# Two projection slabs loaded during normalization, halved weight staging, and a second d_gated buffer in an eight-core transformer layer

## The chip, the cores and the metric

The program runs on all 8 cores of one Trainium2 chip, each core with its own 2048 tokens and no exchange between cores. The metric is device time in microseconds (us), that of the slowest core. PE is TensorE (matmuls), DVE is VectorE, ACT is ScalarE, POOL is GpSimd and SP is SyncE, which here only issues DMA transfers.

## The reference

The input x has shape 2 x 8192 x 1024. Cut to what matters (H = 16 heads, 44 key offsets from 0 to 1536):

```python
xn = _layernorm(x)
# branch 1, attention over a fixed set of key offsets, then a gated FFN
xa = _rmsnorm(xn, norm1_scale)
q, k, v = split(xa @ w_qkv)
alpha = softmax(q . k[t - offset] * scale + pos_bias)
out = sum_o alpha * v[t - offset]
gate = sigmoid(xa @ w_gate + b_gate)
r1 = xn + out * gate @ w_out
xn2 = _rmsnorm(r1, norm2_scale)
r2 = r1 + silu(xn2 @ w_ffn_gate) * (xn2 @ w_ffn_up) @ w_ffn_down
# branch 2, five matrices with 4096 hidden units
h = silu(xn @ w1.T * w1_s) * (xn @ w2.T * w2_s)
h = gelu(h @ h1.T * h1_s)
h = gelu(h @ h2.T * h2_s)
return x + r2 + h @ w3.T * w3_s
```

## The kernel before

A core holds its 2048 tokens and 1536 tokens ahead of them (the halo that the keys and values need), 3584 in all, as columns: 7 blocks of 512. Features lie on the partitions, 8 chunks of 128. The work is a row of stages, each closed by `barrier()`, at which every engine waits for all counters of all engines and transfers.

1. Normalization (`p0_load`, `p0_stats`, `p0_rows`, `p0_apply`, lines 290 to 388). For each block, x is loaded twice: as float32 through ACT's queue into `s_x32` (L298) and, converted to bf16, through POOL's queue into `s_xb` (L302). DVE squares `s_xb` (L311), PE sums columns (L316, L320), DVE works out mean and variance in single rows (L329 to L349), PE spreads them over the partitions (L351 to L354), and DVE applies them in 24 instructions (L365, L368, L370), into `s_xa` (kept in SBUF) and `s_xnb` (stored to `d_xn`, L375). The buffers are double. The loads of block b+2 wait for the application of block b. On DVE the order is: apply block b, rows of block b+1 (13 us), squares of block b+2 (which wait for its `s_xb`), apply block b+1. Ahead of this stage SP issues 16 transfers that replicate the position table in DRAM (`d_grep`, L259).
2. Projections (L426 to L517). Weights come in slabs of 1024 x 512, in the order K (two slabs), Q (two), gate (two), V (two). `p1_slab` (L417 to L424) loads a slab as float32, 2 MB, on SP's queue into the one buffer `s_w832`, and DVE casts it to bf16 into the one buffer `s_w8` (L421). The load waits until the cast before it has read `s_w832`; the cast waits until the last matmul of the slab before it has read `s_w8`. PE's first matmul of a slab waits for the cast (L442 for K and Q, L472 for the gate, L500 for V). `p1_slab` is called at the top of each slab's loop, so on SP the load stands behind the stores of the slab before it (Q stores to `d_q` at L454, the gate to `d_gate` at L489), and the cast stands on DVE behind all evacuations of that slab.
3. Attention, 16 query tiles with 16 heads each. It ends with the output in `d_gated`.
4. Output projection (L753 to L882): 4 blocks of 512 tokens. At its start, POOL issues 144 small loads of scale columns (L781 to L787, semaphore qC2), and ACT's queue loads `wout` in two halves through `s_wo32`, each cast by DVE (L798). For each block, SP loads 1 MB of `d_gated` into the one buffer `s_g4` (L810) and 1 MB of `d_xn` (L815). PE transposes 32 tiles of it (L826) and DVE copies each out of PSUM (L830), PE multiplies by `wout` (L842), DVE adds the residual (L848) and writes the normalized result (L878). The first L878 waits for all of qC2. The load at L810 waits for all matmuls of the block before it, and in block 0 also for both casts of `wout`.
5. FFN of branch 1 (L890 to L1000).
6. Branch 2 in two halves of 1024 tokens; all its matmuls are at L1048.

DVE and ACT execute their instructions in program order, and every DVE instruction waits for the one before it through the counter `vC`. A queue's issues stand in program order too, so a transfer whose wait isn't met holds back those behind it. `tM`, `vC` and `sC` count PE's, DVE's and ACT's milestones.

Of the kernel before, what the change touches and what calls it, by code (L numbers as in the profile page):

```python
# [15 lines left out]
D = 1024  # L16
# [67 lines left out]
def build_nc(offsets, tap=None, upto=99, p2sub=99):  # L84
# [180 lines left out]

    st0b = ExitStack()
# [491 lines left out]
    s_g4 = sb("s_g4", [128, 4 * D], BF16, st3b)  # L758
    g43 = s_g4[:, :].rearrange("p (n d) -> p n d", n=4)
# [30 lines left out]
    p2_end_t = tM.n  # L790
    wo_half_v = []
# [15 lines left out]
    p2_end_v = vC.n  # L807
    p2_end_s = sC.n
    for blk in range(4):
        DA(qG4, lambda s, blk=blk: s.dma_start(  # L810
            g43[:, :, :],
            d_gated.ap().rearrange("n p d -> p n d")[:, blk * 4:(blk + 1) * 4, :]),
           waits=[(tM, tM.n)] + ([(vC, p2_end_v)] if blk == 0 else []))
        g4q = qG4.n
# [5 lines left out]
        for ttl in range(4):  # L820
            for c in range(8):
# [4 lines left out]
                T(lambda t, ttl=ttl, c=c, pt=pt: t.transpose(  # L826
# [8 lines left out]
        gT_ms = vC.n  # L835
        for oc in range(8):
# [362 lines left out]
```

How the kernel before makes its waits and increments, by code:

```python
    def emit(self, eng, fn, incs=(), waits=()):  # L54
        lst = self.q[eng]
        for (c, v) in waits:
            if v > 0:
                lst.append(lambda e, _h=c.h, _v=v: e.wait_ge(_h, _v))
        ivals = []
        for (c, k) in incs:
            c.n += k
            ivals.append((c.h, k))
        def run(e, _fn=fn, _iv=tuple(ivals)):
            inst = _fn(e)
            for (_h, _k) in _iv:
                inst = inst.then_inc(_h, _k)
        lst.append(run)
# [2 lines left out]
def _finish(nc, P, dma_sems):  # L72
    for c_ in dma_sems.values():
        if c_.n > 0:
            P.emit("sync", lambda s, _h=c_.h, _v=c_.n: s.wait_ge(_h, _v))
    with nc.Block() as blk:
        blk.tensor(lambda t: [f(t) for f in P.q["tensor"]])
        blk.vector(lambda v: [f(v) for f in P.q["vector"]])
        blk.scalar(lambda s: [f(s) for f in P.q["scalar"]])
        blk.gpsimd(lambda g: [f(g) for f in P.q["gpsimd"]])
        blk.sync(lambda s: [f(s) for f in P.q["sync"]])
# [2 lines left out]
def build_nc(offsets, tap=None, upto=99, p2sub=99):  # L84
# [109 lines left out]
    def barrier():  # L194
        vals = [(tM, tM.n), (vC, vC.n), (sC, sC.n)]
        vals += [(c, c.n) for c in _dma_sems.values()]
        for eng in ("tensor", "vector", "scalar", "gpsimd", "sync"):
            for (c, v) in vals:
                if v > 0:
                    P.emit(eng, lambda e, _h=c.h, _v=v: e.wait_ge(_h, _v))
# [863 lines left out]
           waits=[(tM, tM.n)])  # L1064
        xhq = qXH.n
        P.q["tensor"].append(lambda t, _v=xhq: t.wait_ge(qXH.h, _v))
```

## Time and profile before

| | us |
|---|---|
| median of three runs | 5027.04 |
| lowest and highest run | 4921.33, 5434.43 |
| the profiled execution | 4936.44 |
| its span on the slowest core (core 3) | 4934.6 |
| spans of the eight cores | 4888.8 to 4934.6 |

The profile comes from one execution. The span runs from the first to the last instruction of the core; 1.8 us of the execution's time lie outside it. PE is busy 79% of the span, DVE 21%, ACT 13%, POOL 6%. In a list of instructions or of waits each row has its line in the kernel; the bracket at the end of a timeline row is the idle time of that engine just before, and what ended it. "PEclk" is the clock that TensorE was granted, as a share of 2.4 GHz: 0.50 is 1.2 GHz. POOLq, SPq and ACTq are the queues from which transfers are issued.

### The profile page before, as it was taken

What the parts mean: (1) busy time and instruction counts of PE and PEld (TensorE: products, weight loads), DVE (VectorE), ACT (ScalarE), POOL (GpSimd) and SP (SyncE); (2) the same over time, 40 slices, a digit from 0 to 9 for tenths busy, and PEclk for the clock granted to TensorE, in tenths of its full rate; (3) what the DMA queues carried; (4) which work ended last, traced back from release to release, by engine and by line L of the source; (5) the groups of instructions that cost most, each with busy time, mean ns of one, the idle gap of its engine ahead of it and who ended that gap; (6) DMA issues with size and microseconds to landing.
All of it is one profiled execution on the core that took longest, in us unless ns stands there. A gap on an engine that the chain in (4) does not pass through costs nothing.

```text
span 4934.6 us, 53307 instructions; the slowest of 8 cores (4888.8 to 4934.6 us)
## 1 busy us (share of the span) xinstructions
PE 3903.3 (79%) x19714; PEld 1853.8 (38%) x19714; DVE 1043.8 (21%) x2047; ACT 663.2 (13%) x802; POOL 283.2 (6%) x310
## 2 busy tenths in 40 slices
PE   1227666555555457998898999999989899999999
PEld 0003222444444223443343444444434344444444
DVE  2663233555555341030011000000011200000001
ACT  0000010444444101100110000000002000000000
POOL 0000000000000600000010000000001000000000
PEclk8558887555555568999999999999999899999999
DMA  5421221000000224206466656555575666665657
GB/s 125 102 77 60 75 79 44 15 21 15 21 15 17 80 77 77 35 1 141 98 77 81 83 71 80 74 75 79 82 153 73 85 75 79 73 81 70 84 71 145
DMA packets 481888, 353.37 MB, mean 72 GB/s; under 512 B 41427, under 2 KB 438740, under 8 KB 479588
## 3 DMA queue, kind: packets, MB, share of 16 engines
q0 software_dynamic: 396064, 216.62, 34.0%
q1 hardware_dynamic: 77236, 114.46, 7.5%
q10 hardware_dynamic: 8336, 18.87, 1.3%
q8 instruction: 164, 2.69, 0.2%
q14 instruction: 88, 0.72, 0.1%
HBM read 513.43 MB, written 53.54 MB: 115 GB/s over the span
## 4 chain that ended last, share of the span: by engine, by line
PE 69%; DVE 12%; DMA 9%; issue 4%; POOL 2%; ACT 1%; DVEq 1%; SPq 1%; another core or an unknown queue 0%; ACTq 0%; POOLq 0%
PE p L1048 49%; DVE s_at L678 4%; PE p_f L982 3%; PE p_f L923 3%; PE p_f L947 3%; PE p_B L653 3%; DMA s_xb<-xT 3%; PE p_gm L442 3%; PE p_gm L500 2%; PE p_av L700 1%; DVE s_b L614 1%; DMA d_gate<-s_evq 1%; DMA s_hs<-h1T 1%; PE p_o L842 1%; DVEq L58 1%
## 5 line engine op out<-in xcount | busy, mean ns | idle before, releaser
L1048 PE MATMUL p<-s_hb,s_hs 128*128 128x512 bf16 x6144 | 1335.2, 380 | 44.9 <-DMA s_hs<-w1T 18.9
L1048 PE MATMUL p<-s_ha,s_hs 128*128 128x512 bf16 x5120 | 1113.8, 381 | 44.5 <-DMA s_hs<-h1T 38.5
L1048 PEld LDWEIGHTS p<-s_hb,s_hs 128*128 128x128 bf16 x6144 | 600.2, 98 | 779.9 <-issue 69.8
L1048 PEld LDWEIGHTS p<-s_ha,s_hs 128*128 128x128 bf16 x5120 | 502.5, 98 | 655.8 <-issue 57.4
L1106 DVE SCALAR_TENSOR_TENSOR s_oo<-p,s_s,s_rr 128x1024 f32<-128x1024 f32 x16 | 20.5, 1284 | 2006.4 <-PE p L1048 1936.5
L700 PE MATMUL p_av<-s_V,s_at 128*128 128x65 bf16 x2048 | 193.5, 235 | 281.9 <-DVE s_at L678 280.4
L664 ACT ACTIVATE s_E<-p_B,s_negB 128x512 bf16<-128x512 f32 x512 | 351.8, 687 | 422.3 <-PE p_B L653 352.3
L700 PEld LDWEIGHTS p_av<-s_V,s_at 128*128 128x128 bf16 x2048 | 125.5, 118 | 374.0 <-issue 374.0
L678 DVE TENSOR_TENSOR s_at<-s_E,s_MT 128x512 bf16<-128x512 bf16 x512 | 217.9, 426 | 171.9 <-DVE s_at L678 56.2
L653 PE MATMUL p_B<-s_qt,s_K 64*128 64x128 bf16 x2048 | 253.9, 307 | 0.0
L442 PE MATMUL p_gm<-s_xa,s_w 128*128 128x512 bf16 x704 | 163.2, 397 | 58.7 <-DVE s_w L421 58.7
L653 PEld LDWEIGHTS p_B<-s_qt,s_K 64*128 64x128 bf16 x2048 | 197.6, 138 | 28.5
L1086 ACT ACTIVATE s_ha<-p,s_sh 128x1024 bf16<-128x1024 f32 x64 | 71.2, 1113 | 815.8 <-PE p L1048 815.8
L1086 ACT ACTIVATE s_hb<-p,s_sh 128x1024 bf16<-128x1024 f32 x64 | 71.3, 1114 | 784.8 <-PE p L1048 784.8
L923 PE MATMUL p_f<-s_xn,s_wga 128*128 128x512 bf16 x704 | 153.8, 382 | 22.1 <-DMA s_wga<-wfg 22.1
L982 PE MATMUL p_f<-s_hatt,s_wd 128*128 128x512 bf16 x704 | 155.0, 384 | 18.9 <-DMA s_wd<-wfd 18.9
L1075 DVE SCALAR_TENSOR_TENSOR s_ha<-p,s_s,s_ha 128x1024 bf16<-128x1024 f32 x64 | 82.2, 1284 | 408.4 <-PE p L1048 408.4
L351 PE MATMUL p_b<-s_row,s_onesf 1*128 1x512 f32 x14 | 14.3, 1121 | 188.8 <-DVE s_row L349 188.8
L947 PE MATMUL p_f<-s_xn,s_wga 128*128 128x512 bf16 x704 | 153.8, 382 | 2.2 <-ACT s_hatt L932 2.2
L1069 ACT ACTIVATE s_ha<-p,s_s 128x1024 bf16<-128x1024 f32 x64 | 71.3, 1113 | 499.4 <-PE p L1048 499.4
L442 PEld LDWEIGHTS p_gm<-s_xa,s_w 128*128 128x128 bf16 x704 | 71.0, 101 | 152.0 <-issue 77.3
L500 PE MATMUL p_gm<-s_w,s_xa 128*128 128x512 bf16 x448 | 102.6, 393 | 20.5 <-DVE s_w L421 20.3
(108 smaller groups left out, 1754.8 us busy)
## 6 DMA issues: line engine op xcount, KB each, us to landing
s_hs<-h1T POOLq DMA_DIRECT2D x32, 2048.0 KB, 19.1
s_hs<-h2T POOLq DMA_DIRECT2D x32, 2048.0 KB, 17.2
s_hs<-w1T POOLq DMA_DIRECT2D x32, 512.0 KB, 5.9
s_hs<-w2T POOLq DMA_DIRECT2D x32, 512.0 KB, 5.9
s_hs<-w3T POOLq DMA_DIRECT2D x8, 2048.0 KB, 19.6
s_x<-xT ACTq DMA_DIRECT2D x7, 2048.0 KB, 15.9
s_w<-wqkv SPq DMA_DIRECT2D x6, 2048.0 KB, 8.2
d_grep<-d_gtab SPq DMA_DIRECT2D x16, 512.0 KB, 43.3
```

The costliest lines, as they stand in the source:

```text
L442: T(lambda t, oc4=oc4, kc=kc, b0=b0, b=b, p=p: t.matmul(p[:, b * 512:(b + 1) * 512], w83[:, kc, oc4 * 128:(oc4 + 1) * 128], xa3[:, kc, (b0 ...
L500: T(lambda t, tt=tt, kc=kc, p=p: t.matmul(p[:, 0:512], xa3[:, kc, tt * 128:(tt + 1) * 128], w83[:, kc, :], start=(kc == 0), stop=(kc == 7) ...
L653: T(lambda t, jj=jj, ktile=ktile, g=g, r0=r0, pB=pB, q3=q3: t.matmul(pB[:, jj * 128:(jj + 1) * 128], K3[r0:r0 + 64, g, ktile * 128:(ktile ...
L664: SE(lambda s, pB=pB, par=par, hx=hx, bi=bi: s.activation(s_E[par][:, hx * HW2:(hx + 1) * HW2], pB[:, hx * HW2:(hx + 1) * HW2], AF.Exp, bi ...
L678: V(lambda v, h=h, par=par, hx=hx: v.tensor_tensor(s_at[par][:, hx * HW2:(hx + 1) * HW2], s_E[par][:, hx * HW2:(hx + 1) * HW2], MT3[:, h, ...
L700: T(lambda t, jj=jj, ktile=ktile, h=h, pav=pav: t.matmul(pav[:, 0:65], s_at[par][:, jj * 128:(jj + 1) * 128], V4[:, ktile, h, :], start=(j ...
L923: T(lambda t, oc=oc, kc=kc, b=b, pf=pf: t.matmul(pf[:, b * 512:(b + 1) * 512], wga3[:, kc, oc * 128:(oc + 1) * 128], xn23[:, kc, b * 512:( ...
L947: T(lambda t, oc=oc, kc=kc, b=b, pf=pf: t.matmul(pf[:, b * 512:(b + 1) * 512], wga3[:, kc, oc * 128:(oc + 1) * 128], xn23[:, kc, b * 512:( ...
L982: T(lambda t, oc=oc, kc=kc, b=b, pf=pf: t.matmul(pf[:, b * 512:(b + 1) * 512], wd3[:, kc, oc * 128:(oc + 1) * 128], ha3[:, kc, b * 512:(b ...
L1048: T(lambda t, o2=o2, kc=kc, b=b, pp=pp, src3=src3, sl3=sl3, n_kc=n_kc: t.matmul(pp[:, b * 512:(b + 1) * 512], sl3[:, kc, o2 * 128:(o2 + 1) ...
L1075: V(lambda v, oc=oc, pp=pp: v.scalar_tensor_tensor(h53[:, oc, :], pp[:, :], s_s2[:, oc:oc + 1], h53[:, oc, :], ALU.mult, ALU.mult), waits= ...
L1086: SE(lambda s, oc=oc, pp=pp: s.activation(dst3[:, oc, :], pp[:, :], AF.Gelu, scale=ssc[:, oc:oc + 1]), waits=[(tM, fm)])
```

## The change

Three things are changed.

- `p1_slab` works with two bf16 buffers, `s_w80` and `s_w81`, which take turns, and with one float32 staging buffer of half a slab (`s_w832`, 128 x 4 x 512). A slab is now two loads of 1 MB and two casts of half the size. Each load waits for the cast before it (`cast_prev`), so the second load of a slab waits for its first cast. The first cast of a slab waits for the matmuls that used the same bf16 buffer two slabs ago.
- The two K slabs are loaded and cast in the normalization stage: `p1_slab` is called after `p0_apply(0)` and after `p0_apply(1)`. For this the buffers are allocated ahead of those of normalization. The other six slabs are called where they were.
- In the output projection `s_g4` becomes two buffers. Block 0 and block 1 are loaded at the start, block 2 and 3 at the top of block 1 and 2. Each load waits for the load before it, and instead of all matmuls for the transposes that read its buffer last (`tr_ms`). The counters `p2_end_v` and `p2_end_s` are taken ahead of the casts of `wout`, so that neither the first load nor the first transpose waits for them.

```diff
+    p1w = {"cast_prev": 0, "mms_done": [0, 0], "idx": 0}
+
+    def p1_slab(src_slab):
+        si = p1w["idx"] & 1
+        p1w["idx"] += 1
+        for hf in range(2):
+            DA(qWS, lambda s, src_slab=src_slab, hf=hf: s.dma_start(
+                w8323[:, :, :], src_slab[:, hf * 4:(hf + 1) * 4, :]),
+               waits=[(vC, p1w["cast_prev"])])
+            wq = qWS.n
+            V(lambda v, si=si, hf=hf: v.tensor_copy(
+                s_w8[si][:, hf * 2048:(hf + 1) * 2048], s_w832[:, :]),
+              waits=[(qWS, wq)] + ([(tM, p1w["mms_done"][si])] if hf == 0 else []))
+            p1w["cast_prev"] = vC.n
+        return si, vC.n
...
         p0_apply(blk)
+        if blk <= 1:
+            k_pre.append(p1_slab(wqkv_v[:, :, D + blk * 512: D + (blk + 1) * 512]))
...
-            cast_v = p1_slab(wqkv_v[:, :, base_col + wh * 512: base_col + (wh + 1) * 512])
+            if not is_q:
+                si, cast_v = k_pre[wh]
+            else:
+                si, cast_v = p1_slab(wqkv_v[:, :, base_col + wh * 512: base_col + (wh + 1) * 512])
+            w83 = w83v[si]
...
-            p1w["mms_done"] = tM.n
+            p1w["mms_done"][si] = tM.n
...
+    def g4_load(blk, fw):
+        DA(qG4, lambda s, blk=blk: s.dma_start(
+            g43v[blk & 1][:, :, :],
+            d_gated.ap().rearrange("n p d -> p n d")[:, blk * 4:(blk + 1) * 4, :]),
+           waits=fw)
+        g4qs[blk] = qG4.n
+
+    g4_load(0, [(tM, tM.n), (vC, p2_end_v)])
+    g4_load(1, [(tM, tM.n), (qG4, qG4.n)])
     for blk in range(4):
-        DA(qG4, lambda s, blk=blk: s.dma_start(
-            g43[:, :, :],
-            d_gated.ap().rearrange("n p d -> p n d")[:, blk * 4:(blk + 1) * 4, :]),
-           waits=[(tM, tM.n)] + ([(vC, p2_end_v)] if blk == 0 else []))
-        g4q = qG4.n
+        if blk >= 1 and blk + 1 < 4:
+            g4_load(blk + 1, [(tM, tr_ms[blk - 1]), (qG4, qG4.n)])
+        g43 = g43v[blk & 1]
+        g4q = g4qs[blk]
```

DVE at the end of block 0's application, in the normalization stage, before. `s_xa` is the normalized x, `s_row` the single-row values of the next block; a bracket names the counters waited for.

```order
L365 TENSOR_TENSOR s_x<-s_x,p_b 128x512 [waits vC]
L368 TENSOR_TENSOR s_xnb<-s_x,p_b 128x512 [waits vC]
L370 SCALAR_TENSOR_TENSOR s_xa<-s_x,s_g,p_b 128x512 [waits vC]
L329 COPY s_row<-p_s1b 1x512 [waits vC,tM]
L331 COPY s_row<-p_s2b 1x512 [waits vC]
L333 TENSOR_SCALAR s_row<-s_row 1x512 [waits vC]
L334 TENSOR_TENSOR s_row<-s_row 1x512 [waits vC]
```

The same place on DVE in the changed kernel (L396 to L401 is the application, L288 the cast in `p1_slab`, L360 and up the rows):

```order
L396 TENSOR_TENSOR s_x<-s_x,p_b 128x512 [waits vC]
L399 TENSOR_TENSOR s_xnb<-s_x,p_b 128x512 [waits vC]
L401 SCALAR_TENSOR_TENSOR s_xa<-s_x,s_g,p_b 128x512 [waits vC]
L288 CAST s_w<-s_w 128x2048 [waits vC,qWS] x2
L360 COPY s_row<-p_s1b 1x512 [waits vC,tM]
L362 COPY s_row<-p_s2b 1x512 [waits vC]
L364 TENSOR_SCALAR s_row<-s_row 1x512 [waits vC]
```

Two casts of half a slab, each waiting for a load on qWS, stand between the application of block 0 and the rows of block 1; the same pair stands behind the application of block 1.

DVE where the K slabs end and the first Q slab begins, before. `s_K` rows are evacuations of K, `s_evq` rows those of Q.

```order
L458 CAST s_K<-p_gm1 128x512 [waits vC,tM]
L458 CAST s_K<-p_gm0 128x1024 [waits vC,tM]
L458 CAST s_K<-p_gm1 128x1024 [waits vC,tM]
L458 CAST s_K<-p_gm0 128x1024 [waits vC,tM]
L458 CAST s_K<-p_gm1 128x512 [waits vC,tM]
L421 CAST s_w8<-s_w832 128x4096 [waits vC,qWS,tM]
L451 TENSOR_SCALAR s_evq<-p_gm0 128x1024 [waits vC,tM]
```

The same place in the changed kernel (L471, L288, L464):

```order
L471 CAST s_K<-p_gm1 128x1024 [waits vC,tM]
L471 CAST s_K<-p_gm0 128x1024 [waits vC,tM]
L471 CAST s_K<-p_gm1 128x512 [waits vC,tM]
L288 CAST s_w80<-s_w832 128x2048 [waits vC,qWS,tM]
L288 CAST s_w80<-s_w832 128x2048 [waits vC,qWS]
L464 TENSOR_SCALAR s_evq<-p_gm0 128x1024 [waits vC,tM]
L464 TENSOR_SCALAR s_evq<-p_gm1 128x1024 [waits vC,tM,qES]
L464 TENSOR_SCALAR s_evq<-p_gm0 128x1024 [waits vC,tM,qES]
```

One cast of 4096 columns has become two of 2048, at the same place in the order: behind all evacuations of the slab before.

SP from the position table to the stores of Q and the gate, before:

```order
L259 DMA d_grep<-d_gtab 128x2048 x16
L418 DMA s_w<-wqkv 128x8x512 x3
L454 DMA d_q<-s_evq 128x1024 x8
L418 DMA s_w<-wqkv 128x8x512
L454 DMA d_q<-s_evq 128x1024 x8
L418 DMA s_w<-wgate 128x8x512
L489 DMA d_gate<-s_evq 128x512 x16
```

The same stretch of SP in the changed kernel (L284 is the load in `p1_slab`):

```order
L259 DMA d_grep<-d_gtab 128x2048 x16
L284 DMA s_w<-wqkv 128x4x512 x6
L467 DMA d_q<-s_evq 128x1024 x8
L284 DMA s_w<-wqkv 128x4x512 x2
L467 DMA d_q<-s_evq 128x1024 x8
L284 DMA s_w<-wgate 128x4x512 x2
L503 DMA d_gate<-s_evq 128x512 x16
```

Each load of 2 MB has become a pair of 1 MB. Of the six ahead of the first Q store, four are those of the K slabs and directly follow the table transfers; the pairs behind the stores stand where the single loads stood.

## Rows read from the trace of the kernel before

**Rows 1.** Busy time by stretch; columns in the first row.
```profile
core 3: us, PE busy (x) PEld busy (x) DVE busy (x) ACT busy (x) POOL busy (x), PEclk, DMA share, GB/s
0.00:384.30 384.30, 79.41 (x154) 24.93 (x154) 200.17 (x254) 22.72 (x30) 12.72 (x18) 0.64 0.42 100
384.30:812.80 428.50, 328.29 (x1408) 139.41 (x1408) 151.88 (x253) 21.42 (x33) 0.00 (x0) 0.88 0.17 59
2360.00:4934.60 2574.60, 2479.33 (x11405) 1116.21 (x11402) 126.90 (x98) 217.63 (x195) 176.57 (x136) 0.98 0.62 85
```

**Rows 2.** Waits of PE between 384 and 830 us.
```profile
PE p_gm L442 <- DVE s_w L421: 58.7, 4, 36.8
PE p_gm L472 <- DVE s_w L421: 31.3, 2, 16.0
PE p_gm L500 <- DVE s_w L421: 20.3, 2, 16.2
```

**Rows 3.** Timeline of SP, DVE and PE in the projections.
```profile
384.27 66.41 SPq L418 DMA_DIRECT2D s_w<-wqkv  x3
393.07 2.29 DVE L421 CAST s_w<-s_w 128x4096 bf16<-128x4096 f32 x1 [14.85 <-DMA s_w<-wqkv]
395.51 51.39 PE L442 MATMUL p_gm<-s_xa,s_w 128*128 128x512 bf16 x224 [36.83 <-DVE s_w L421]
447.95 2.29 DVE L421 CAST s_w<-s_w 128x4096 bf16<-128x4096 f32 x1 [0.24 <-DVE s_K L458]
450.39 29.90 PE L442 MATMUL p_gm<-s_xa,s_w 128*128 128x512 bf16 x125 [3.48 <-DVE s_w L421]
550.54 9.68 PE L442 MATMUL p_gm<-s_xa,s_w 128*128 128x512 bf16 x34 [14.92 <-DVE s_w L421]
```

**Rows 4.** Busy time by stretch behind one slab change; columns as in rows 1.
```profile
450.40:457.00 6.60, 6.60 (x18) 2.40 (x19) 0.14 (x1) 0.00 (x0) 0.00 (x0) 0.58 0.85 303
457.00:502.00 45.00, 44.65 (x207) 20.05 (x205) 16.88 (x16) 0.00 (x0) 0.00 (x0) 1.00 0.01 3
```

**Rows 5.** DMA issues of the page: transfer, issuer, count, KB each, median us to landing.
```profile
s_w<-wqkv SPq DMA_DIRECT2D x6, 2048.0 KB, 8.2
d_grep<-d_gtab SPq DMA_DIRECT2D x16, 512.0 KB, 43.3
s_xb<-xT POOLq DMA_DIRECT2D x7, 1024.0 KB, 18.6
d_xn<-s_xnb POOLq DMA_DIRECT2D x7, 1024.0 KB, 11.1
s_g<-d_gated SPq DMA_DIRECT2D x4, 1024.0 KB, 5.8
s_xnb<-d_xn SPq DMA_DIRECT2D x4, 1024.0 KB, 5.2
```

**Rows 6.** Timeline of SP, DVE and POOL in the normalization stage.
```profile
24.76 41.26 SPq L259 DMA_DIRECT2D d_grep<-d_gtab  x16
131.54 0.68 DVE L329 COPY s_row<-p_s1b 1x512 f32<-1x512 f32 x1 [0.24 <-DVE s_xa L370]
132.76 0.88 POOL L302 DMA_DIRECT2D s_xb<-xT  x1
152.16 2.29 DVE L311 TENSOR_TENSOR s_xnb<-s_xb 128x4096 bf16<-128x4096 bf16 x1 [7.75 <-DMA s_xb<-xT]
194.24 2.29 DVE L311 TENSOR_TENSOR s_xnb<-s_xb 128x4096 bf16<-128x4096 bf16 x1 [7.10 <-DMA s_xb<-xT]
```

**Rows 7.** Busy time by stretch between two blocks; columns as in rows 1.
```profile
140.00:153.00 13.00, 6.22 (x8) 2.07 (x9) 3.92 (x5) 1.35 (x2) 0.00 (x0) 0.50 0.93 219
```

**Rows 8.** Timeline of DVE in the output-projection stage.
```profile
1672.47 0.22 DVE L830 COPY s_gT<-p_t 128x128 bf16<-128x128 bf16 x1 [8.12 <-PE p_t L826]
1732.30 6.70 DVE L878 SCALAR_TENSOR_TENSOR s_xn<-s_r,s_g,p_bc 128x512 bf16<-128x512 f32 x8 [20.88 <-DMA s_sh<-sh2v]
1739.17 0.22 DVE L830 COPY s_gT<-p_t 128x128 bf16<-128x128 bf16 x1 [0.17 <-DVE s_xn L878]
```

More of the change, by code:

```diff
@@ L264, in build_nc @@
     stg.close()
+    st1b = ExitStack()
+    s_w8 = [sb("s_w80", [128, 8 * 512], BF16, st1b, side="right"),
+            sb("s_w81", [128, 8 * 512], BF16, st1b, side="right")]
+    w83v = [t[:, :].rearrange("p (k o) -> p k o", k=8) for t in s_w8]
+    s_w832 = sb("s_w832", [128, 4 * 512], F32, st1b, side="right")
+    w8323 = s_w832[:, :].rearrange("p (k o) -> p k o", k=4)
+    s_evq = sb("s_evq", [128, 1024], BF16, st1b, side="right")
+    s_gt32 = sb("s_gt32", [128, 512], F32, st1b, side="right")
+    s_vc = sb("s_vc", [128, 1], F32, st1b, side="right")
+    wSL = DS("wSL")
+    qWS = DS("qWS")
+    qES = DS("qES")
+    p1w = {"cast_prev": 0, "mms_done": [0, 0], "idx": 0}
[12 more added lines that the diff above has]
+        return si, vC.n
+    wqkv_v = wqkv.ap().rearrange("(k p) o -> p k o", p=128)
+    wgate_v = wgate.ap().rearrange("(k p) o -> p k o", p=128)
+    k_pre = []
     st0b = ExitStack()
@@ L441, in build_nc @@
                         for b in range(gn):
-                            T(lambda t, oc4=oc4, kc=kc, b0=b0, b=b, p=p: t.matmul(
+                            T(lambda t, oc4=oc4, kc=kc, b0=b0, b=b, p=p, w83=w83: t.matmul(
                                 p[:, b * 512:(b + 1) * 512],
@@ L463, in build_nc @@
                     pi ^= 1
-            p1w["mms_done"] = tM.n
+            p1w["mms_done"][si] = tM.n
     for wh in range(2):
-        cast_v = p1_slab(wgate_v[:, :, wh * 512:(wh + 1) * 512])
+        si, cast_v = p1_slab(wgate_v[:, :, wh * 512:(wh + 1) * 512])
+        w83 = w83v[si]
         for tt in range(QT_N):
@@ L471, in build_nc @@
             for kc in range(8):
-                T(lambda t, tt=tt, kc=kc, p=p: t.matmul(
+                T(lambda t, tt=tt, kc=kc, p=p, w83=w83: t.matmul(
                     p[:, 0:512],
@@ L491, in build_nc @@
                waits=[(sC, sv)])
-        p1w["mms_done"] = tM.n
+        p1w["mms_done"][si] = tM.n
     for wh in range(2):
-        cast_v = p1_slab(wqkv_v[:, :, 2 * D + wh * 512: 2 * D + (wh + 1) * 512])
+        si, cast_v = p1_slab(wqkv_v[:, :, 2 * D + wh * 512: 2 * D + (wh + 1) * 512])
+        w83 = w83v[si]
         for tt in range(NT):
@@ L499, in build_nc @@
             for kc in range(8):
-                T(lambda t, tt=tt, kc=kc, p=p: t.matmul(
+                T(lambda t, tt=tt, kc=kc, p=p, w83=w83: t.matmul(
                     p[:, 0:512],
@@ L757, in build_nc @@
     st3b = ExitStack()
-    s_g4 = sb("s_g4", [128, 4 * D], BF16, st3b)
-    g43 = s_g4[:, :].rearrange("p (n d) -> p n d", n=4)
+    s_g4 = [sb("s_g40", [128, 4 * D], BF16, st3b), sb("s_g41", [128, 4 * D], BF16, st3b)]
+    g43v = [t[:, :].rearrange("p (n d) -> p n d", n=4) for t in s_g4]
     s_wo = sb("s_wo", [128, 8 * 1024], BF16, st3b)
@@ L790, in build_nc @@
     p2_end_t = tM.n
+    p2_end_v = vC.n
+    p2_end_s = sC.n
     wo_half_v = []
@@ L825, in build_nc @@
                     fw += [(vC, p2_end_v), (sC, p2_end_s)]
-                T(lambda t, ttl=ttl, c=c, pt=pt: t.transpose(
+                T(lambda t, ttl=ttl, c=c, pt=pt, g43=g43: t.transpose(
                     pt[:, :], g43[:, ttl, c * 128:(c + 1) * 128], s_id[:, :]),
@@ L835, in build_nc @@
         gT_ms = vC.n
+        tr_ms[blk] = tM.n
         for oc in range(8):
```

26 lines of the change are left out of this document (2 added, 24 removed).

## The prediction

> **What bounds the kernel now.** I read the busy time by stretch first. More than half of the span, 2574.6 of 4934.6 us, is branch 2, where PE is busy 2479 us at a granted clock of 0.98 [rows 1]. The change doesn't touch it. What it touches is the normalization stage (384.3 us, PE busy 79, DVE busy 200, so neither is full), the projections (428.5 us, PE busy 328) and the output projection. The reader should see in the first row that DVE is idle for 184 us: this stage is a chain of loads and DVE work, not an engine at its limit.
>
> Next the waits of PE in the projections [rows 2]. Eight slabs cost PE 58.7 + 31.3 + 20.3 = 110.3 us of idle time, and 36.8 of that is the first, which lies mostly ahead of the barrier. So the most that a perfect staging could give is about 80 us and what the clock gives back. The timeline splits them into two kinds [rows 3]. K slab 0 is issued at 384.27, cast at 393.07, and PE starts at 395.51: everything exposed. K slab 1 was loaded behind PE's back; only the cast is seen (3.48 us idle). The second Q slab is exposed again (14.92 us), since its load stands on SP behind the stores of Q.
>
> Last, the DVE timeline around the new places: the end of block 0's application in normalization [rows 6] and the start of the output projection [rows 8].
>
> **K slabs: what is removed.** PE can start right behind the barrier, at 384.3 + 0.2 instead of 395.51: -11.0 us. At K slab 1 the idle 3.48 us go, but for some 0.2: -3.3. Behind that gap the granted clock is 0.58 for 6.6 us, in which 18 matmuls run [rows 4]; at the 207 in 45 us of the next row, 0.217 us each, they would take 3.9: -2.7 more, as PE then never pauses. Together -17.0.
>
> **The other six slabs: two loads in a row.** A half slab's cast costs 1.15 (half of 2.29 [rows 3]). The second load waits for the first cast, and DVE reaches that first cast only behind the last evacuation of the slab before. So the second bf16 buffer gives nothing here: the order of DVE, not the buffer, holds the cast back. For the first Q slab and the second V slab, whose load used to be hidden, a whole 1 MB load comes to stand in front of PE. One MB alone lands after 5.2 or 5.8 us, 2 MB after 8.2 [rows 5]. I take 5.2 and 0.4 for two more hand-overs: +5.6 each. For the second Q, both gate and the first V slab the sum is 2 x 5.2 + 0.4 - 8.2 = +2.6 each. In all 2 x 5.6 + 4 x 2.6 = +21.6. The bounds: 4.1 for 1 MB, if a load had no fixed part (half of 8.2), gives 2 x 4.5 + 4 x 0.4 = +10.6; 5.8 gives 2 x 6.2 + 4 x 3.8 = +27.6. The clock behind these gaps is low already before, so nothing changes there. The projections together: -17.0 + 21.6 = +4.6 (-6.4 to +10.6).
>
> The Trainium skill speaks against this edit too: DMA: Bandwidth & Descriptors, "Anatomy of one DMA", gives every transfer a fixed cost of about 2 us beside its bytes at 436 GB/s. An estimate by that page is 4.4 us for 1 MB and 6.8 for 2 MB, so +2.0 for a pair in place of one. The trace's 8.2 us for 2 MB is slower than that, and this sum goes by the trace.
>
> **Normalization: what is added.** The first half load of K slab 0 is issued behind the 16 table transfers, at about 66 us (24.76 + 41.26 [rows 6]), and has landed long before DVE's cast at 131. Its cost is traffic while the loads of the first two blocks are still waited for: 1 MB at 219 GB/s [rows 7] is 4.8 us if all of it is ahead of them, 0 if it comes last. I take 2.4.
>
> Then the cast pair between the application of block 0 and the rows of block 1. DVE casts, SP issues the second half, DVE waits, casts, and only then begins the rows. Everything on DVE is queued behind this wait: rows, squares, application. Through the rows, PE's broadcast and ACT's logarithm wait too. At the same moment the loads of block 2 and the store of block 0 are issued (132.76 and close by [rows 6]), so this load isn't alone: the DMA share is 0.93 in that stretch [rows 7]. The trace has no such load. From below it is 5.2 (alone), from above 43.3 (the table transfers in their own deep queue) [rows 5]. I take 11.1, that of the `d_xn` store, which is of the same size and in the same company. The pair then costs 2 x 1.15 + 0.24 + 0.4 + 11.1 = 14.0. DVE had 7.75 us of idle time here, waiting for `s_xb` [rows 6], so the rows finish 14.0 - 7.75 = 6.3 us too late. But `s_xb` itself comes later: the second half and then the first half of K slab 1 are 2 MB of new traffic ahead of it, up to 9.6 us. The later of the two counts, and I take 8, between 6.3 and 9.6. Behind block 1 the same: 14.0 - 7.10 = 6.9 against 4.8 of traffic, so 6.9. Nothing recovers this later, since the loads of block b+2 wait for the end of application b. Normalization: 2.4 + 8 + 6.9 = +17.3. With a load of 5.2 the pair costs 8.1, and the stage 0.4 + 1.0 = +1.4; the far end is a rival below.
>
> **Output projection: what seems saved.** The first load of `d_gated` no longer waits for the casts of `wout`, so the 8.12 us that DVE idles before the first copy go [rows 8]. But at the end of block 0 DVE waits 20.88 us for the small scale loads, which POOL issues from the start of the stage whatever block 0 does. That cover takes the 8 us, and any delay of the `wout` load by the new traffic beside it; if it were gone, 8 us would be gained. For blocks 1 to 3 the load was hidden already: the first copy of block 1 starts 0.17 us behind the last L878 [rows 8]. PE has transposed ahead and waits for DVE, not for the load. I take 0 (bounds -8 and 0). SP's load of `d_xn` for block 0 now also stands behind both `d_gated` loads, and lies under the same cover.
>
> **Sum.** +17.3 + 4.6 + 0 = +21.9 us on 4936.4, the profiled execution's time (span 4934.6 and 1.8 around it): 4958 us, 0.4% more. The middle of the three runs before is 5027, 91 above the profiled one, and the lowest 15 below it. This spread is larger than the effect, and the range makes room for it. A measurement of this kernel can tell about 2%, some 99 us, from no change.
>
> **Rivals.**
>
> *The loads in normalization hide.* If the second half lands in 5.2 us, the pair fits the idle time, and with cheap halves in the projections the sum is +1.4 - 6.4 = -5.0: 4931 us. For it: a lone 1 MB load on SP's queue does land in 5.2 us [rows 5]. Against it: the load is issued exactly when the others are. 16%.
>
> *The load gets a quarter of the engines.* Four transfers at once: `s_x32`, `s_xb`, the store and the slab. A fourth of 219 GB/s is 55 GB/s, 19.2 us for 1 MB, close to the 18.6 of `s_xb` [rows 5]. The pairs then cost 22.1 each, the stage 14.4 + 15.0 + 4.8 = +34.2, the whole +38.8: 4975 us. The Trainium skill has this as its rule (DMA: Bandwidth & Descriptors, "Queues, rings and completion order"): each DMA engine goes round the queue rows it has work for, a packet at a time. Against an equal share in bytes: the store lands in 11.1 beside longer transfers. 15%.
>
> *Slower than before by about 2%: the wait is as deep as in the table's queue.* If the two waits on qWS in normalization take 43.3 us, they cost 46.2 - 7.75 and 46.2 - 7.10, together 77.6. With 4.8 and the upper bound of the projections, 10.6, this is +93: 5029 us. It passes 2% when one load takes 47 us or more. Against it: the last table transfer, issued by 66 us, has landed by about 110, so SP's queue is empty at 131, and the 43.3 come from 16 transfers of which each also writes DRAM. 5%.
>
> *It does what it seems meant to do.* If each cast ran while PE still worked on the slab before, the waits inside the projections would vanish: 110.3 less the 25.6 ahead of the barrier (36.8 - 11.2), and 2.7 of clock for seven changes, about -104: 4832 us. Against it stands the order of DVE, in which the casts of the six later slabs haven't moved. 2%.
>
> My forecast has the remaining 62%: within 2% of before and slightly slower. Slower by over 2% is most of the third rival and a little for a shift of the whole: 4%. Faster by over 2% is the last rival: 2%. The rest, 94%, is within 2%. The range runs from 4915 (the first rival in a run as low as the lowest one) to 5040 (the forecast in a run as far up as the middle one of before).
>
> **What would show it.** In the profile after, the first cast in normalization should follow the application at once, the second with 8 to 20 us of idle time for DMA in front of it; the rows of block 1 start some 14 us late, and the barrier falls near 402 instead of 384. PE's first K matmul then follows within 0.5 us, and there is no gap at K slab 1. At the first Q slab PE's idle time should rise from 3.5 to about 9 us, at the second from 14.9 to about 17.5. The first L878 of the output projection should still end a wait for the scale loads. The prediction is wrong if the normalization stage ends before 390 or after 425, if the gaps at the later slabs shrink, or if branch 2 changes its length by more than 10 us.

## The result, and the profile after

The changed kernel is 1.0% slower than the one before: the ratio is 1.0101 (95% interval 1.0082 to 1.0121), some 50 us. Some executions of every kernel, before and after, are several per cent longer at a lower clock on one half of the cores or on both; the ratios, times and stretches here leave such executions, or such cores, out. Of ten executions of the changed kernel seven remain, of 4966.72 to 4976.82 us with a median of 4969.25. Between the two profiled executions the difference is 30.3 us (4936.4 and 4966.7). Between their cores it is 40.7 in the mean, since the slowest core of before stood 26 us above the mean of its eight, that of after 16. The forecast was +21.9 us.

The stretches, each from the start of one marked instruction to that of the next, mean over the eight cores, in us:

| stretch | before | after | difference | forecast |
|---|---|---|---|---|
| normalization, to the issue of the last `d_xn` store | 376.9 | 404.8 | +27.9 | +17.3 |
| from there to the first K matmul | 16.4 | 5.6 | -10.8 | -11.0 |
| projections, to the last V matmul | 412.7 | 431.6 | +18.9 | +15.6 |
| attention, to its last score matmul | 819.2 | 817.1 | -2.1 | 0 |
| output projection, to the first write of xn2 | 97.2 | 99.9 | +2.7 | 0 |
| rest of it and FFN | 671.7 | 672.8 | +1.1 | 0 |
| branch 2, from its first matmul to the end | 2514.2 | 2517.2 | +2.9 | 0 |

Busy time by stretch in the kernel after, on its slowest core (core 0), to set beside [rows 1]:

```profile
core 0: us, PE busy (x) PEld busy (x) DVE busy (x) ACT busy (x) POOL busy (x), PEclk, DMA share, GB/s
0.00:414.20 414.20, 77.08 (x154) 24.40 (x154) 204.38 (x258) 22.72 (x30) 13.54 (x18) 0.64 0.42 103
414.20:845.30 431.10, 320.93 (x1408) 137.86 (x1408) 148.23 (x257) 21.43 (x33) 0.00 (x0) 0.89 0.15 49
```

DVE has only 4.2 us more to do in the first stretch (the casts), but the stretch is 30 us longer. So this isn't work, it is waiting. The timeline of DVE in normalization after, the counterpart of [rows 6]:

```profile
131.60 1.23 DVE L288 CAST s_w<-s_w 128x2048 bf16<-128x2048 f32 x1 [0.17 <-DVE s_xa L401]
150.97 1.23 DVE L288 CAST s_w<-s_w 128x2048 bf16<-128x2048 f32 x1 [18.15 <-DMA s_w<-wqkv]
152.44 0.68 DVE L360 COPY s_row<-p_s1b 1x512 f32<-1x512 f32 x1 [0.24 <-DVE s_w L288]
165.18 2.29 DVE L342 TENSOR_TENSOR s_xnb<-s_xb 128x4096 bf16<-128x4096 bf16 x1 [0.24 <-DVE s_row L380]
190.36 1.23 DVE L288 CAST s_w<-s_w 128x2048 bf16<-128x2048 f32 x1 [0.17 <-DVE s_xa L401]
208.32 1.23 DVE L288 CAST s_w<-s_w 128x2048 bf16<-128x2048 f32 x1 [16.74 <-DMA s_w<-wqkv]
222.90 2.29 DVE L342 TENSOR_TENSOR s_xnb<-s_xb 128x4096 bf16<-128x4096 bf16 x1 [0.24 <-DVE s_row L380]
```

The first cast follows the application at once. Before the second, DVE waits 18.15 us, and at the next block 16.74. The rows of block 1 start at 152.44, against 131.54 before: 20.9 us late, of which the 7.75 us of waiting for `s_xb` give some back (that wait is now 0.24). The squares stand at 165.18 against 152.16 before. These rows are from the slowest core. Over the eight cores the first wait is 15.2 to 18.2 us, 16.6 in the mean, and the second 14.3 to 17.9 us, 16.0 in the mean.

Behind the squares there is a second cost. DVE's first instruction of the application, in the kernel after and at the same place before (core 3):

```profile
170.82 0.69 DVE L396 TENSOR_TENSOR s_x<-s_x,p_b 128x512 f32<-128x512 f32 x1 [3.35 <-PE p_b L385]
154.69 0.69 DVE L365 TENSOR_TENSOR s_x<-s_x,p_b 128x512 f32<-128x512 f32 x1 [0.24 <-DVE s_xnb L311]
```

Before, PE spread the rows over the partitions while DVE waited for `s_xb`. Now that wait is gone, and DVE waits 3.35 us for PE instead of 0.24. It is so at blocks 1 and 2, on every core: 6.2 us in all.

How long the transfers take there is seen in the list of DMA issues of the kernel after (transfer, issuer, count, KB each, median us to landing), beside [rows 5], and in the stretch of the wait:

```profile
s_w<-wqkv SPq DMA_DIRECT2D x12, 1024.0 KB, 5.4
s_xb<-xT POOLq DMA_DIRECT2D x7, 1024.0 KB, 20.3
d_xn<-s_xnb POOLq DMA_DIRECT2D x7, 1024.0 KB, 11.5
s_g<-d_gated SPq DMA_DIRECT2D x4, 1024.0 KB, 12.3
```

```profile
133.00:151.00 18.00, 0.00 (x0) 0.00 (x0) 0.03 (x1) 0.00 (x0) 1.18 (x2) 0.50 0.91 257
```

The median of 5.4 us for a half slab hides two of 18.0 and 16.6, those issued at 133 and 191 (over all cores these landed after 14.2 to 18.0 us), and one of 46.9, the first, which is issued behind the table transfers. In the 18 us from 133 to 151 PE and ACT do nothing, DVE 0.03 us, and the DMA engines move 257 GB/s for four transfers. In the same window before, with three transfers, it was 230 GB/s (core 3).

The trace also has every DMA packet with its queue, its start and its size, and on core 0 these show how the four transfers divide the time. They come through three queues, since the store and `s_xb` are both issued by POOL. The slab's first packet starts 6.2 us after the issue (4.0 to 6.2 us over the cores at this load, 1.0 us for the load behind the barrier, which is alone); until 139 only `s_x32` moves. From 141 to 147, when all three queues are at work, POOL's moves 242 packets, SP's 260 and ACT's 259. So each queue gets nearly the same number of packets, whatever they hold: the slab's 1 MB is 512 packets of 2 KB, that of the store 256 packets of 4 KB.

In the projections, SP, DVE and PE at the barrier, at the first Q slab and at the second, beside [rows 3]:

```profile
414.21 0.37 SPq L284 DMA_DIRECT2D s_w<-wqkv  x1
414.39 10.79 PE L455 MATMUL p_gm<-s_xa,s_w 128*128 128x512 bf16 x43 [25.93 <-DMA d_xn<-s_xnb]
...
513.65 1.23 DVE L288 CAST s_w<-s_w 128x2048 bf16<-128x2048 f32 x1 [0.24 <-DVE s_K L471]
514.96 0.37 SPq L284 DMA_DIRECT2D s_w<-wqkv  x1
520.10 1.23 DVE L288 CAST s_w<-s_w 128x2048 bf16<-128x2048 f32 x1 [5.22 <-DMA s_w<-wqkv]
521.47 8.82 PE L455 MATMUL p_gm<-s_xa,s_w 128*128 128x512 bf16 x29 [8.86 <-DVE s_w L288]
...
563.17 1.23 DVE L288 CAST s_w<-s_w 128x2048 bf16<-128x2048 f32 x1 [6.10 <-DMA s_w<-wqkv]
569.69 1.23 DVE L288 CAST s_w<-s_w 128x2048 bf16<-128x2048 f32 x1 [5.29 <-DMA s_w<-wqkv]
571.06 9.23 PE L455 MATMUL p_gm<-s_xa,s_w 128*128 128x512 bf16 x35 [19.39 <-DVE s_w L288]
```

PE starts 0.18 us behind SP's first issue after the barrier. At the first Q slab one can read the series of steps: cast, issue, 5.2 us of load, cast, and PE's 8.86 us of idle time, where it was 3.5. At the second Q slab both loads are in front of PE: 19.39 where it was 14.92. PE's waits in the projections of the kernel after, beside [rows 2]:

```profile
PE p_gm L486 <- DVE s_w L288: 37.3, 2, 19.2
PE p_gm L515 <- DVE s_w L288: 28.7, 2, 19.1
PE p_gm L455 <- DVE s_w L288: 28.3, 2, 19.4
PE p_gm L455 <- DMA d_xn<-s_xnb: 25.9, 1, 25.9
```

Six slabs cost PE 94.3 us. Before, the same six cost 110.3 less the two K slabs (36.8 and 3.5), 70.0.

In the output projection of the kernel after, DVE at the end of block 0 and at the start of block 1, beside [rows 8]:

```profile
1763.30 6.70 DVE L905 SCALAR_TENSOR_TENSOR s_xn<-s_r,s_g,p_bc 128x512 bf16<-128x512 f32 x8 [22.98 <-DMA s_sh<-sh2v]
...
1770.17 0.22 DVE L856 COPY s_gT<-p_t 128x128 bf16<-128x128 bf16 x1 [0.17 <-DVE s_xn L905]
```

The small scale loads still end the wait, and block 1 still starts 0.17 us behind block 0's last write.

### The profile page after: what moved, and what is told of

Its sections match the earlier page's. It is cut to its first block, busy times and chain, and to the rows that moved or that the text cites. A ratio compares the mean times of both kernels' runs of the same rounds, so it can differ in the third digit from the quotient of the medians.

```text
span 4965.2 us, 53354 instructions; the slowest of 8 cores (4927.8 to 4965.2 us)
## 1 busy us (share of the span) xinstructions
PE 3883.7 (78%) x19714; PEld 1850.6 (37%) x19714; DVE 1044.3 (21%) x2055; ACT 663.1 (13%) x802; POOL 284.0 (6%) x310
## 4 chain that ended last, share of the span: by engine, by line
PE 67%; DVE 12%; DMA 11%; issue 4%; POOL 2%; ACT 1%; DVEq 1%; SPq 1%; another core or an unknown queue 0%; ACTq 0%; POOLq 0%
PE p L1075 47%; DVE s_at L693 4%; PE p_f L950 3%; PE p_f L1009 3%; PE p_f L974 3%; PE p_B L668 3%; PE p_gm L455 2%; PE p_gm L515 2%; DMA s_xb<-xT 2%; PE p_av L715 1%; DMA s_w<-wqkv 1%; DMA s_hs<-h1T 1%; DMA s_xx<-xT 1%; DMA d_gate<-s_evq 1%; DVE s_b L629 1%
## 5 line engine op out<-in xcount | busy, mean ns | idle before, releaser
L382 PE MATMUL p_b<-s_row,s_onesf 1*128 1x512 f32 x14 | 14.3, 1121 | 224.9 <-DVE s_row L380 224.9
```

## The experiments

Four kernels ran first, then four more. The theory at that point: DVE's wait for the second half load in normalization is the loss, and the load is slow because of its company.

**1. The same loads, with a whole block of time for each (e_four).** One half cast at the end of each of the blocks 0 to 3, its load issued at the end of the block before.

```diff
-        if blk <= 1:
-            k_pre.append(p1_slab(...))
+        if blk <= 3:
+            cv = p1_cast(blk >> 1, blk & 1)
+            if blk < 3:
+                p1_load(k_half(blk + 1), (blk + 1) & 1)
```

> The changed kernel with the four half casts of the K slabs spread over the ends of blocks 0 to 3 in normalization, so that each half load has a whole block (some 40 us) to land before DVE asks for it. Same bytes, same number of casts; all else as in the changed kernel. Theory (it is DVE's wait for the second half, 16.7 to 18.2 us twice, that lengthened normalization by 28 us): DVE never waits for qWS by more than 1 us, the casts of 1.23 us fit into the 6 to 7 us in which DVE waits for s_xb, and only traffic is left, at most 4.8 us at each of three places: normalization 5 us longer than before (0 to 14), the kernel 14 to 28 us below the changed one, ratio to before 1.004 to 1.008. Rival (it is the added 4 MB of traffic, whatever waits for it): normalization stays 25 to 30 us longer than before and the ratio stays at 1.010.

Measured: ratio 1.0047 (1.0023 to 1.0072). Normalization took 386.0 us in the mean over cores, 9.1 more than before and 18.8 less than after. DVE's timeline, on the slowest core:

```profile
131.47 1.23 DVE L300 CAST s_w<-s_w 128x2048 bf16<-128x2048 f32 x1 [0.17 <-DVE s_xa L413]
155.09 2.29 DVE L354 TENSOR_TENSOR s_xnb<-s_xb 128x4096 bf16<-128x4096 bf16 x1 [9.65 <-DMA s_xb<-xT]
```

DVE doesn't wait for the slab any more, but its wait for `s_xb` has grown (at block 2 8.8 us in the mean over cores, 7.3 before) though it comes to it 1.4 us later. DVE's wait for PE's broadcast is back at 0.24. So two thirds of the loss, 18.8 of 27.9 us, are the wait for the slab and what it uncovers, and one third stays with the loads spread out. That is nearer to the upper than to the lower end of what I had allowed for traffic.

**2. Halving alone (e_projonly).** The two calls in normalization are taken out, and all eight slabs are staged in halves at the top of their loops; the new output projection stays.

```diff
-        if blk <= 1:
-            k_pre.append(p1_slab(...))
...
-            if not is_q:
-                si, cast_v = k_pre[wh]
-            else:
-                si, cast_v = p1_slab(...)
+            si, cast_v = p1_slab(...)
```

> The changed kernel without the two calls in normalization: all eight slabs are loaded and cast at the top of their own loops, in halves and into two bf16 buffers. Theory (halving puts a second load of 5.4 us in front of PE, and the second bf16 buffer gives nothing, since DVE reaches the cast behind the last evacuation): normalization as before within 2 us; K slab 0 and four others 2.6 us longer, K slab 1, the first Q and the second V slab 5.6 us longer, in all 4 + 5 = about 30 us on top of before (5 x 2.6 + 3 x 5.6 = 29.8), ratio 1.006. Rival (two bf16 buffers let casts run while PE works on the slab before): PE's waits for the casts sum to less than before (under 110 us), ratio 1.000 or below.

Measured: ratio 1.0079 (1.0054 to 1.0103). On cores 0 to 3, from the last store of normalization to the last V matmul it took 460.1 us, against 429.7 on the same cores before, +30.4 (expected 29.8), and normalization was as before (374.3 us against 374.9). PE's waits for the casts, on core 0:

```profile
PE p_gm L450 <- DVE s_w L288: 74.9, 4, 38.9
PE p_gm L481 <- DVE s_w L288: 36.5, 2, 19.1
PE p_gm L510 <- DVE s_w L288: 28.7, 2, 19.2
```

140.1 us in place of 110.3 (core 3). The halved staging costs what was worked out with the second bf16 buffer giving nothing. The buffer wasn't tried without the halving, so this rests on the sum and on the place of the casts behind the evacuations in DVE's order.

**3. The output projection alone (e_g4only).** The kernel before, with the two `s_g4` buffers and their loads and waits from the change.

> The kernel before with only the output-projection part of the change (two s_g4 buffers, loads issued early, the first load and transpose not waiting for the wout casts). Theory (the gain at the start is covered by the wait for the small scale loads, and blocks 1 to 3 were hidden): 0 us, ratio 0.999 to 1.001, and the first L878 still ends a wait for the scale loads, of 26 to 30 us in place of 20.9. Rival 1 (the prefetch pays): 8 us at the start and up to 5 us in each block, ratio 0.995 to 0.998. Rival 2 (the two early loads delay the wout and scale loads): the stage 2 to 5 us longer, ratio 1.0005 to 1.001.

Measured: ratio 1.001 (0.9988 to 1.0032), so no gain of 0.2% or more. The stretch to the first write of xn2 was 98.4 us against 97.2. The row of that write:

```profile
1731.17 6.70 DVE L890 SCALAR_TENSOR_TENSOR s_xn<-s_r,s_g,p_bc 128x512 bf16<-128x512 f32 x8 [22.86 <-DMA s_sh<-sh2v]
```

On the same core (core 5) it was 17.7 us before:

```profile
DVE s_xn L878 <- DMA s_sh<-sh2v: 17.7, 1, 17.7
```

The wait is 5.2 us longer there, and 3.9 in the mean over cores (22.7 against 18.9), where some 8 were expected. The missing part has two places. The copies stand behind the casts of `wout` on DVE, and these come later too: on core 5 the two waits for their loads are 14.90 and 9.46 us, before 12.03 and 9.51 on the same core, so some 3 of the 8 us are gone before the copies start. What is left falls under the wait for the scale loads, whose landing sets the first write in both kernels, here 1.2 us later than before.

**4. Casts moved into the slab before (e_mid).** As e_four, and in the projections the next slab's first load is issued at the top of a slab, its first cast and second load stand after 3/8 of the slab's units, the second cast after 6/8.

```diff
+    def slab_step(n, u, units):
+        if not 2 <= n + 1 < 8:
+            return
+        if u == (units * 3) // 8:
+            p1_cast((n + 1) & 1, 0)
+            p1_load(slab_src(n + 1), 1)
+        elif u == (units * 6) // 8:
+            ready[n + 1] = ((n + 1) & 1, p1_cast((n + 1) & 1, 1))
```

> As e_four, and in the projections the load of the next slab's first half is issued at the top of a slab, its cast and the load of the second half stand after three eighths of the slab's units, the second cast after six eighths. Output projection as in the changed kernel. Theory (the order of DVE is what kept the casts behind each slab, and with it moved the second bf16 buffer pays): PE's waits for s_w in the projections fall from 85 us behind the barrier to under 5, TensorE's clock doesn't fall between slabs, the projections are 85 to 104 us shorter than before, the kernel 80 to 100 us, ratio 0.980 to 0.984. Rival (casts between evacuations hold PE's two PSUM buffers back): each of 12 casts costs up to 1.2 us of PE, and the loads share the queue with stores, so the gain is under 60 us, ratio 0.988 or more.

Measured: ratio 0.9876 (0.9859 to 0.9894). Normalization was again 10.3 us longer than before, the projections 63.1 shorter (349.6 in place of 412.7), and the barrier's 10.9 are saved too. PE's waits in the projections, on the slowest core:

```profile
PE p_gm L532 <- DVE s_gt L540: 24.1, 25, 2.9
PE p_gm L498 <- DVE s_evq L507: 6.5, 4, 2.8
PE p_gm L564 <- DVE s_V L578: 1.8, 2, 0.9
PE p_gm L564 <- DVE s_gt L540: 1.3, 2, 0.8
PE p_gm L532 <- DVE s_w L300: 1.2, 1, 1.2
```

```profile
392.00:742.00 350.00, 310.60 (x1382) 133.52 (x1383) 144.96 (x247) 21.42 (x33) 0.00 (x0) 0.97 0.19 64
```

The waits for `s_w` fall to 1.2 us and the clock stays at 0.97, as the theory has it. But the gain, 74 us with the barrier, missed the expected 85 to 104 us by 11 or more, and the ratio lies between the theory's 0.984 and the rival's 0.988, nearer to the rival. New waits of PE for evacuations came up: 33.7 us, against the 15.2 that the kernel before had for the gate. The casts and the stores held up by a slab load on SP are the candidates; this wasn't taken apart. Loads and casts were moved together, so the kernel doesn't tell what either is worth alone.

**5. A smaller second load (e_six_two).** The K slabs are split 6 + 2 chunks.

```diff
-            k_pre.append(p1_slab(wqkv_v[:, :, D + blk * 512: D + (blk + 1) * 512]))
+            k_pre.append(p1_slab(wqkv_v[:, :, D + blk * 512: D + (blk + 1) * 512], ((0, 6), (6, 8))))
```

> The changed kernel with the K slabs split 6 + 2 of their 8 chunks in place of 4 + 4, so that the load for which DVE waits in normalization is 0.5 MB in place of 1 MB (the staging buffer is 12 KB per partition for it). Equal-share theory (four transfers share the DMA engines, each getting about a quarter of 219 GB/s): the wait in front of the second cast falls from 16.7 and 18.2 us to 8 to 11, normalization ends 12 to 18 us before that of the changed kernel. Rival (SP's load is served only once the others are through, whatever its size): the wait stays at 15 to 18 us, and normalization is shorter by less than 5.

Measured in one execution, 4961.04 us. One execution gives no ratio worth comparing, here and in experiment 6; the waits and the stretches decide. The two waits on the slowest core:

```profile
144.62 0.69 DVE L288 CAST s_w<-s_w 128x1024 bf16<-128x1024 f32 x1 [11.57 <-DMA s_w<-wqkv]
195.88 0.69 DVE L288 CAST s_w<-s_w 128x1024 bf16<-128x1024 f32 x1 [10.65 <-DMA s_w<-wqkv]
```

This core has nearly the shortest of them. Over the eight cores the waits are 11.0 to 14.3 and 10.3 to 13.8 us, 12.5 and 11.8 in the mean, against 16.6 and 16.0 in the kernel after. Half the bytes take a quarter off the wait, not a half. So the load isn't held back until the others are through, but an equal share of the bytes isn't what it gets either: by the packets, its first one still starts 3.8 to 5.7 us after the issue, and only what follows gets shorter. The waits together are 8.5 us shorter, normalization 6.3 in the mean, where the theory had 12 to 18 and the rival less than 5. The other 2 us lie ahead of the first pair (squares of block 1 0.9 us later) and in the later waits for `s_xb` (1.1 us longer in all).

**6. The same wait in less company (e_late).** The calls stand behind the rows of blocks 1 and 2, when only `s_xb` is still on its way.

```diff
         p0_rows(blk)
+        if 1 <= blk <= 2:
+            k_pre.append(p1_slab(wqkv_v[:, :, D + (blk - 1) * 512: D + blk * 512]))
```

> The changed kernel with the two K slab calls moved from behind the application of blocks 0 and 1 to behind the rows of blocks 1 and 2, some 13 us later, when the load of s_x32 and the store of d_xn have nearly landed and only s_xb is still on its way. Theory (the 17 us come from the company of three other transfers): the second half, issued beside one other transfer, lands in 7 to 10 us, DVE waits 7 to 9, and of each pair's 12 us some 7 lie in the time in which DVE waits for s_xb anyway: normalization 8 to 14 us longer than before, 14 to 20 shorter than in the changed kernel. Rival (a load on SP takes 17 us in this stage whenever it is issued): waits of 15 us or more, normalization as long as in the changed kernel.

Measured in one execution, 4937.45 us. DVE on the slowest core:

```profile
145.14 1.23 DVE L288 CAST s_w<-s_w 128x2048 bf16<-128x2048 f32 x1 [0.17 <-DVE s_row L380]
155.69 1.23 DVE L288 CAST s_w<-s_w 128x2048 bf16<-128x2048 f32 x1 [9.32 <-DMA s_w<-wqkv]
157.15 2.29 DVE L342 TENSOR_TENSOR s_xnb<-s_xb 128x4096 bf16<-128x4096 bf16 x1 [0.24 <-DVE s_w L288]
```

The same 1 MB load on the same queue now keeps DVE waiting for 9.32 us (8.28 at the second; 8.8 and 7.8 in the mean over cores). Normalization was 8.2 us longer than before and 19.7 shorter than after. Of the 19.7, 16.1 are shorter waits for the slab and 6.2 the broadcast of the rows, which now runs while DVE waits; later waits for `s_xb` take 1.7 back. Only the place of the calls was changed, so what made the load so slow in the kernel after is the other transfers.

**7. Loads when the DMA engines stand still (e_quiet).** As e_mid, but the half loads of the K slabs also wait until `s_xb` of the next block has landed. Each is issued ahead of the application of the block whose end has its cast; the calls of e_mid, the first ahead of the stage and the others a block earlier, are gone.

```diff
+        if blk <= 3:
+            p1_load(k_half(blk), blk & 1, [(wXB[(blk + 1) & 1], p0["wq"][(blk + 1) & 1])])
         p0_apply(blk)
```

> As e_mid, but each half load of the K slabs in normalization waits until s_xb of the next block has landed (one more semaphore wait on SP), so it runs while DVE applies a block and the DMA engines stand still. Theory (in e_four and e_mid the 9 to 10 us by which normalization is longer than before are traffic: s_xb lands 2 to 3 us later in each of three blocks): s_xb lands as before, 17 to 19 us after its issue, DVE's idle time before the squares falls to 5 to 6.5 us, normalization within 3 us of before, the kernel 7 to 9 us below e_mid, ratio 0.986. Rival (it is the four casts on DVE, 1.5 us each, and some delay of another kind): normalization stays 5 to 10 us longer than before, ratio as e_mid, 0.9876.

Measured: ratio 0.9857 (0.9840 to 0.9875), median 4855.14 us. Normalization took 375.8 us, 1.1 less than before and 11.4 less than e_mid. DVE's waits for `s_xb`, on the slowest core:

```profile
153.81 2.29 DVE L354 TENSOR_TENSOR s_xnb<-s_xb 128x4096 bf16<-128x4096 bf16 x1 [8.14 <-DMA s_xb<-xT]
197.19 2.29 DVE L354 TENSOR_TENSOR s_xnb<-s_xb 128x4096 bf16<-128x4096 bf16 x1 [6.96 <-DMA s_xb<-xT]
239.39 2.29 DVE L354 TENSOR_TENSOR s_xnb<-s_xb 128x4096 bf16<-128x4096 bf16 x1 [5.86 <-DMA s_xb<-xT]
```

This core's waits lie mostly above the 5 to 6.5 us that were expected; the mean over cores is 6.5, 5.2 and 4.9 us (7.3, 6.7 and 5.9 before). Each half load lands after 5.3 to 6.3 us in the mean. The four casts are still there and cost nothing, so the third that e_four had left was traffic, and it goes when the same bytes move a little later. Between e_mid and e_quiet the ratios' intervals overlap; it is the stretch that tells them apart.

**8. As e_quiet, with the output projection of before (e_quiet_oldg4).**

> As e_quiet, with the output projection of the kernel before (one s_g4, loads where they were). In the four kernels with the changed output projection the time from the last attention matmul to the first L878 was 98.4 to 99.9 us against 97.2 before, a mean over cores. Theory (the change of the output projection gives nothing, its early loads cost 1 to 2 us by delaying the small scale loads): this stretch comes back to 97 to 98 us, the kernel 1 to 2 us below e_quiet, within the noise. Rival (the prefetch gives something once the rest is faster): this kernel 3 us or more above e_quiet.

Measured: ratio 0.9855 (0.9835 to 0.9874). The stretch to the first write of xn2 was 96.4 us against 99.0 in e_quiet, and the whole is the same within the noise. In the eight kernels with the new output projection this stretch was 98.4 to 100.5 us, in the two with the old one 97.2 and 96.4. So that part of the change costs about 2 us; which of its pieces does wasn't tried. e_quiet and e_quiet_oldg4 beat both kernels by some 70 and 120 us.

## Why the prediction was right and wrong

**The wait in normalization: the step that failed.** The prediction took 11.1 us for the second half load, the landing time of the `d_xn` store, because that is of the same size and in the same company. It took 18.0 and 16.6 us, 16.5 and 15.9 in the mean over cores. The store was the wrong row to go by, twice over. Its 11.1 is a median of seven, and the last two have no loads beside them (5.1 and 5.4 us); in this very place, behind block 0, the store took 13.1 us before. And equal size in equal company isn't equal time: the store (14.5 us after) needs half as many packets, and the slab's first packet starts 4.0 to 6.2 us late. Why it starts so late isn't known.

The rival nearest to it was the quarter share, with 19.2 us. Experiments 5 and 6 bear out that the wait goes down with the bytes and with the company, but not the share itself: three queues had work and not four, they shared nearly by packets and not by bytes, and half the bytes gave three quarters of the wait. The equal packet counts agree with what the prediction cites from the Trainium skill (DMA: Bandwidth & Descriptors, "Queues, rings and completion order"), that each DMA engine goes round the queue rows it has work for, a packet at a time, as far as the trace's packets are the page's. The rival's size was in part luck.

**The cover: a term put at nothing.** The prediction let DVE's idle time for `s_xb`, 7.75 and 7.10 us, pay for the pair in full. That idle time also covered PE's broadcast of the rows, and 3.1 us of it came back at each of the two blocks. In the mean over cores the waits for the slab are 32.7 us, the casts and hand-overs 5.6, the waits for `s_xb` that went -13.6, the broadcasts 6.2, and later waits for `s_xb` are 2.1 shorter: +28.8, where +27.9 was measured, against the 14.9 (8 + 6.9) that the prediction had. With loads of 11.1 the same sum is some 10 us less.

**Traffic ahead of `s_xb`.** With the wait so long, DVE came to `s_xb` later than `s_xb` came (0.24 us of idle time), so the alternative of 9.6 us was never on the path. The 2.4 us allowed for the start were not seen: the squares of block 1 stand at 107.6 us in the mean over cores, at 107.7 before. The mechanism is real, though: experiments 1, 4 and 7 show 9 to 11 us of it once the wait is gone.

**K slabs.** Right. -11.0 at the barrier was -10.8. There is no gap at K slab 1.

**The later slabs.** Right in kind and nearly in size. +5.6 for the first Q slab was +5.4 (8.86 less 3.48); +2.6 for the second was +4.5 (19.39 less 14.92). The projections were +18.9 against -6.0 + 21.6 = +15.6, and experiment 2 gave +30.4 where the same working gives 29.8. That the second bf16 buffer gives nothing as long as the casts stand behind the evacuations is borne out from both sides: by experiment 2, where the sum without a gain comes out, and by experiment 4, where loads and casts stand earlier and the waits fall to 1.2 us. The prediction's estimate from the Trainium skill (DMA: Bandwidth & Descriptors, "Anatomy of one DMA"), 4.4 us for 1 MB and 6.8 for 2 MB, goes by a fit that the page gives for transfers issued from GpSimd. These loads are issued from SP, and alone they landed after 5.0 to 5.5 us for 1 MB and after 7.8 to 8.7 for 2 MB.

**Output projection.** Right that it gives nothing; about 2 us of cost were missed. The reason given, a cover by the wait for the scale loads, holds; some 3 of the 8 us are lost ahead of it, at the casts of `wout`.

**The sum.** +21.9 was forecast. The stretches give +40.7, and the comparison of runs about +50. Of the gap, 10.6 us are the normalization stage, 3.3 the projections, 2.7 the output projection and 2.9 the last stage, which may be chance. Another 9 or so lie between the profiled executions and the comparison, and the spans on record place about half of them. By the mean span of its cores, the profiled execution of the changed kernel was its shortest (4949.0 us, seven others 4950.4 to 4956.1), while that of before was ordinary (4908.3, the mean of nine others too): that mean gives +45. What is left is in the slowest core alone; the base of the forecast, 4936.4, lies above every other such execution of the kernel before (4918.6 to 4928.9).

"Within 2%" and "slightly slower" were right; the size was wrong by a factor of two. That the result lies well inside the range says little, since the range was drawn for the spread of the executions and not for the mechanism. By its own words its upper end should be 5049 (4958 + 91), not 5040. And the 2574.6 us given as branch 2 hold about 50 us of the stage before: its first matmul starts near 2409, which leaves 2525 us and changes nothing in the argument.

## What to carry to other kernels

A load whose data the busiest in-order engine waits for at once must be priced with all queues that have work at that moment, and by its packets, not by its time alone or by that of a neighbour of the same size. Idle time into which new work is put may already cover something else: here it hid 3.1 us of another engine's work at each place. A prefetch has two parts, an early load and an early place for the work that consumes it; a second buffer without the second part gave nothing here, and halving the staging to pay for it makes two latencies out of one. Before moving a wait off one engine, look for a stretch in which the DMA engines stand still: the same 4 MB cost 28 us in pairs at the busy moment, 9 to 10 spread over four blocks, and nothing when each load also waited until the DMA engines were quiet.

## What the runs showed of the hardware that I had not expected

- A 1 MB load from SP's queue landed after 5.4 us in the median and after 14.2 to 18.0 beside three other transfers (16.2 in the mean), and kept DVE waiting for 7.1 to 10.5 us beside one. With 0.5 MB beside three the wait was 10.3 to 14.3 us.
- Of that landing time 3.9 to 6.2 us pass before the load's first packet starts; in the load behind the barrier it is 1.0 us.
- Three queues at work at once moved 242, 260 and 259 packets in 6 us. The share goes nearly by packets, so the queue with the larger packets moves more bytes.
- In the window from 133 to 151 us four transfers moved 257 GB/s, three 230 before. Together the queues gain a little there, while each transfer loses. On the slowest cores the store landed after 14.5 us (13.1 before), the two loads of 2 MB each read from DRAM after 18.4 (16.1) and 22.8 (19.2), the slab's 1 MB after 18.0.
